# Sorted expert blocks: row transposes moved from TensorE and VectorE to DMA, with four operand buffers and six PSUM banks

## The reference

```python
gate = xf @ Wg + bg                                  # xf: 8192 x 128, 8 experts
topv, topi = jax.lax.top_k(gate, 2)
probs = jax.nn.softmax(topv, axis=-1)
comb = jnp.zeros((N, E)).at[jnp.arange(N)[:, None], topi].set(probs)
h = jax.nn.relu(jnp.einsum('nc,ecf->nef', xf, W1) + b1)   # hidden width 512
y = jnp.einsum('nef,efc->nec', h, W2) + b2
out = jnp.einsum('nec,ne->nc', y, comb)
```

## Time and profile before

| | |
|---|---|
| Median of 3 runs | 2232.34 us (2230.03 to 2232.52) |
| The profiled execution's own time | 2230.25 us |
| Its span in the trace | 2228.3 us |
| PE / DVE / ACT / POOL busy, share of span | 78% / 62% / 53% / 40% |
| Phase 8, first load issued to last scatter issued | 1920.52 us to 2175.8 us of the span |

### The profile page before, as it was taken

How to read it: one execution, slowest core, us unless ns; L and a number is a source line. 1 busy time by engine, 2 the same in 40 slices (tenths; PEclk the granted TensorE clock), 3 DMA queues, 4 the chain that set the end, 5 groups by cost and what they waited for, 6 DMA issues and landing times.

```text
span 2228.3 us, 46761 instructions
## 1 busy us (share of the span) xinstructions
PE 1747.8 (78%) x14634; PEld 956.4 (43%) x14634; DVE 1380.8 (62%) x3633; ACT 1190.7 (53%) x1780; POOL 898.8 (40%) x1789
## 2 busy tenths in 40 slices
PE   2968888888866788877999999999995440499990
PEld 2824444444435233333444444444443430277660
DVE  5445565556547777884666666666664650377766
ACT  1446767676754678752444444444445430388770
POOL 1232323232313233342434443444343477466664
PEclk9999999999975899975999999999996555699995
DMA  5099000000010000000000000000003011122227
GB/s 147 1 335 331 0 0 0 0 0 0 0 48 0 10 0 0 0 38 1 1 0 0 0 0 0 0 0 0 0 1 114 29 54 54 58 88 89 88 75 231
DMA packets 59021, 99.89 MB, mean 45 GB/s; under 512 B 8690, under 2 KB 25970, under 8 KB 57908
## 3 DMA queue, kind: packets, MB, share of 16 engines
q1 hardware_dynamic: 47216, 78.87, 10.8%
q0 software_dynamic: 9088, 18.89, 2.5%
q10 hardware_dynamic: 2628, 1.00, 0.2%
HBM read 38.84 MB, written 59.90 MB: 44 GB/s over the span
## 4 chain that ended last, share of the span: by engine, by line
PE 33%; POOL 6%; DVE 5%; issue 4%; ACT 2%; DVEq 2%; DMA 1%; POOLq 1%; ACTq 0%; SPq 0%
PE OP L1657 7%; POOL h_dram L393 5%; PE OP L1952 5%; PE SP L1937 4%; PE M L1616 4%; PE M L1572 3%; PE M L1586 2%; DVE mx L1042 2%; PE SP L1637 2%; PE M L1612 2%; PE M L1607 2%; ACT shared L637 1%; PE OP L1686 1%; PE M L1927 1%; DVE st L1001 1%
## 5 line engine op out<-in xcount | busy, mean ns | idle before, releaser
L656 ACT ACTIVATE pt<-SP 128x1024 f32<-128x1024 f32 (+1 forms) x512 | 459.7, 921 | 364.9 <-PE SP L1637 364.7
L1657 PE MATMUL OP<-pt,vs 128*32 128x256 f32 (+1 forms) x4096 | 434.4, 362 | 15.4 <-ACT pt L656 13.8
L1042 DVE TENSOR_REDUCE mx<-M 128x2 f32<-128x512 f32 (+1 forms) x384 | 257.0, 690 | 118.1 <-PE M L1616 114.9
L1657 PEld LDWEIGHTS OP<-pt,vs 128*32 128x32 f32 x4096 | 177.0, 110 | 182.6 <-issue 51.3
L475 POOL TENSOR_SCALAR_AFFINE_SELECT pt<-pt 128x256 f32<-128x256 f32 x512 | 196.0, 407 | 0.0
L403 POOL DMA_INDIRECT y_dram<-hT,dest x156 | 150.7, 966 | 108.6 <-DVE hT L1309 72.1
L751 ACT ACTIVATE pt<-SP,b 128x512 f16<-128x512 f32 x156 | 107.2, 687 | 143.0 <-PE SP L1937 116.7
L472 POOL TENSOR_TENSOR spare<-ones 128x1 f32<-128x1 f32 x256 | 49.4, 193 | 309.0 <-ACT pt L656 308.8
L1637 PE MATMUL SP<-shared,ksT 32*128 32x256 f16 (+1 forms) x2048 | 172.0, 262 | 2.4 <-ACT ksT L629 1.2
L1616 PE MATMUL M<-ksT,shared 24*128 24x128 f16 (+1 forms) x1024 | 153.5, 250 | 0.0
L442 POOL TENSOR_TENSOR ha<-hT,ones 128x256 f32<-128x256 f32 x64 | 39.6, 619 | 280.1 <-PE M L1572 270.8
(11 more groups left out here) (267 smaller groups left out, 3330.0 us busy)
## 6 DMA issues: line engine op xcount, KB each, us to landing
h_dram<-shared SPq DMA_DIRECT2D x8, 4488.0 KB, 34.3
hT<-h_dram SPq DMA_DIRECT2D x39, 264.0 KB
rows<-g_dram SPq DMA_DIRECT2D x4, 2048.0 KB, 7.1
pt<-y_dram SPq DMA_DIRECT2D x32, 256.0 KB, 3.7
x_sb<-in_x SPq DMA_DIRECT2D x8, 512.0 KB, 8.9
pt<-in_w SPq DMA_DIRECT2D x4, 1024.0 KB, 7.1
out<-x_sb SPq DMA_DIRECT2D x16, 256.0 KB, 3.0
y_dram<-hT,dest POOLq DMA_INDIRECT x156
```

What stands on the lines that cost most here:

```text
L656: act.activation(pt[:, u % 4, :, 0:W], SP[u % 2][:, :, 0:W], ACT.Exp, scale=SCALE).then_inc(s["exp"], 1)
L1042: dve.tensor_reduce(to, M[:, k % 2, :].rearrange("p (j k) -> p j k", j=2 if k < 8 else 4), AX.X, ALU.max).then_inc(s["mred"], 1)
L1657: last = pe.matmul(OP[32 * g:32 * g + 32, j // 2, c + q0:c + T], vs[:, par, k, HG * j + g, :], pt[:, u % 4, i, k * T:k * T + T - q0], star ...
```

## The change

SP now also issues, for each block, four DMAs with `transpose=True`, each of which turns one row group of 128 rows by 256 16-bit numbers (64 KB) from `xg` into the moving operand. TensorE's eight transposes and VectorE's copy are gone. The operand has four buffers instead of two (two more lie in the tensor `st`). Banks 6 and 7, which the transposes used, join banks 0 to 3 in a ring of six for the first products, taken in turn over all pairs (g, f).

In SP's order the transposes of block g - 1 stand behind the load of block g, so also behind that load's wait for `yE`. They wait for the load of their own block, and from the fifth block on until TensorE has done the first products of the block four before.

```diff
-        hg = ksT[:].rearrange("p a j t -> p (a j t)").rearrange("p (k v n) -> p k v n", k=2, v=2)
+        hg = [half.rearrange("p (k v n) -> p k v n", k=2, v=2)[:, k]
+              for half in (ksT[:].rearrange("p a j t -> p (a j t)"), str_[:].bitcast(F16)) for k in range(2)]
...
-        blk_s = sems("blk", 0, "xT xE hid relu lo y yE dst in0 in1 in2 in3 out0 out1 out2 out3 yin0 yin1 yin2 yin3 sum comb done")
+        blk_s = sems("blk", 0, "hid relu lo y yE in0 in1 in2 in3 out0 out1 out2 out3 yin0 yin1 yin2 yin3 sum comb done turn0 turn1 turn2 turn3")
...
+        def hid_bank(i):
+
+            return bank[(0, 1, 2, 3, 6, 7)[i % 6]]
...
+            def turn_rows(g):
+
+                sp.wait_ge(k[f"in{g % 4}"], 16 * (g // 4 + 1))
+                if g >= 4:
+                    sp.wait_ge(k["hid"], F1 * (g - 3))
+                for r in range(4):
+                    sp.dma_start(hg[g % 4][:, :, r * P:(r + 1) * P], xg[:, g % 4, r, 0:D].bitcast(F16),
+                                 transpose=True).then_inc(k[f"turn{g % 4}"], 16)
+
             for g in range(NBLK):
                 row = sp.value_load(browi[0:1, g:g + 1], min_val=0, max_val=HROWS - BLK)
                 if g >= 4:
                     sp.wait_ge(k["yE"], g - 3)
                 sp.dma_start(xg[:, g % 4].rearrange("p n c -> p (n c)"),
                              h_dram[bass.ds(row, BLK), :].rearrange("(p g) c -> p (g c)", g=4)).then_inc(k[f"in{g % 4}"], 16)
+                if g:
+                    turn_rows(g - 1)
+            turn_rows(NBLK - 1)
...
-                        act.activation(hid1[:, g % 2, f, 0, :], bank[f], ACT.Relu, bias=bias, scale=1.0 / WSCALE)
-                        act.activation(relu[:, f, :], bank[f], ACT.Relu, bias=bias,
+                        of = hid_bank(F1 * g + f)
+                        act.activation(hid1[:, g % 2, f, 0, :], of, ACT.Relu, bias=bias, scale=1.0 / WSCALE)
+                        act.activation(relu[:, f, :], of, ACT.Relu, bias=bias,
                                        scale=1.0 / WSCALE).then_inc(k["relu"], 1)
...
-                def take(g):
-
-                    dve.wait_ge(k["xT"], g + 1)
-                    if g >= 2:
-                        dve.wait_ge(k["hid"], F1 * (g - 1))
-                    dve.tensor_copy(hg[:, g % 2].rearrange("p v n -> p (v n)"), bank[6 + g % 2].bitcast(F16)).then_inc(k["xE"], 1)
...
-                take(0)
                 for g in range(NBLK):
                     targets(g)
-                    low(g, 0)
-                    low(g, 1)
-                    low(g, 2)
-                    if g + 1 < NBLK:
-                        take(g + 1)
-                    low(g, 3)
+                    for f in range(F1):
+                        low(g, f)
                     if g:
                         leave(g - 1)
...
-                def take(g):
-
-                    pe.wait_ge(k[f"in{g % 4}"], 16 * (g // 4 + 1))
-                    if g >= 2:
-                        pe.wait_ge(k["xE"], g - 1)
-                    to = bank[6 + g % 2].bitcast(F16).rearrange("p (v g n) -> p v g n", v=2, g=4)
-                    for r in range(4):
-                        for v in range(2):
-                            last = pe.transpose(to[:, v, r, :], xg[:, g % 4, r, v * D // 2:(v + 1) * D // 2].bitcast(F16), ident16[:])
-                    last.then_inc(k["xT"], 1)
-
                 def hidden(g, f, e):
 
                     if f == 0:
-                        pe.wait_ge(k["xE"], g + 1)
-                    if g:
-                        pe.wait_ge(k["relu"], F1 * (g - 1) + f + 1)
+                        pe.wait_ge(k[f"turn{g % 4}"], 64 * (g // 4 + 1))
+                    i = F1 * g + f
+                    if i >= 6:
+                        pe.wait_ge(k["relu"], i - 5)
                     for n, (u, v) in enumerate(PARTS):
-                        last = pe.matmul(bank[f], w16[1][:, 0, u, bass.ds(e * (F1 * P) + f * P, P)], hg[:, g % 2, v, :],
+                        last = pe.matmul(hid_bank(i), w16[1][:, 0, u, bass.ds(e * (F1 * P) + f * P, P)], hg[g % 4][:, v, :],
                                          start=(n == 0), stop=(n == 2))
                     last.then_inc(k["hid"], 1)
...
-                take(0)
                 e0 = None
...
-                    if g + 1 < NBLK:
-                        take(g + 1)
                     hidden(g, 3, e)
```

## The result

The changed kernel takes 2295.22 us in the median (2292.76 to 2299.68), the kernel before on the same chip 2231.19: a ratio of 1.0289, 95% interval 1.027 to 1.0309. It is 64 us slower; forecast were 32 us slower (2263), within a range of 2213 to 2400. The profiled execution took 2293.29 us, its span 2291.5.

What follows compares the result with a forecast made beforehand. It took phase 8 as bound by TensorE's instruction order; after the change late transposes would set a pitch of 6.92 us. -0.9, +28.1 and +4.0 gave +31.2 us: 2261.5, or 2263.5 on the median, range 2213 to 2400.

Steps and rivals of the forecast that it cites:

- TensorE's share: TensorE's order in phase 8: eight transposes cost 0.45 us per block, so 6.14 falls to 5.69; 17.1 us if TensorE binds.
- The banks and the buffers priced at nothing: First products' bank ring and operand buffers: six banks instead of four buy 0; four buffers only loosen how early transposes land.
- VectorE's copy: Copy after TensorE's transposes, 0.683 us, 39 times: removal priced at nothing, since TensorE's 6.14 us cover VectorE's 4.62.
- The release 2.06 us after the end of the block two before: SP's order: transposes stand behind a load that waits for VectorE's `leave`, so they start 2.06 us after that end.
- The sum: Whole kernel: two pitches gain 0.45 each, 36 lose 0.78 each, the start adds 4.0; together +31.2 us.
- The full clock: TensorE, busy 5.69 of 6.92 us (82%), was expected to keep granted clock 1.00, not the 1.2 GHz level.
- x: SP's queue: distance between two transposing issues, taken as 1.26 us from GpSimd's scatter; break-even at 0.74 with y = 2.3.
- y: Time from a block's last transposing issue to its landing, taken as 2.3 us from a 64 KB scatter.
- The corner "x = 1.26, y = 3.7: P = 7.62": Case of scatter-like issues and slow landing: block pitch P of 7.62 us, 1.48 above today.
- The first two pitches: Start of phase 8: the first three loads wait for nothing, so these pitches gain 0.45 us each.
- Cheap transposes: Rival on SP's issues: x = 0.34, y = 2.3, transposes hidden; -15.9 us, 2216.4; chance 0.35.
- "The DMA engines themselves take longer": Rival: DMA engines need longer for a block's transposes than TensorE for the block; about 2392 us; chance 0.20.

Runs made afterwards that it cites:

- none: The changed kernel with the four transposes left out, so first products read whatever lies in the buffers: 2210.30 us, ratio 0.9907 to the kernel before.
- one_early: The changed kernel with one transposing DMA of 256 KB per block, a separate load of the fields and the looser load wait: 2215.51 us, ratio 0.9922.
- four_banks_again: The changed kernel with four banks instead of six in the ring of the first products, on the usual chip: 2297.96 us, ratio 1.029.
- two_buffers: The changed kernel with two operand buffers instead of four, transposes waiting for the first products of the block two before: 2293.98 us, ratio 1.0284.
- early: The changed kernel with SP's load waiting for its buffer's last reader, `targets(g - 4)`, instead of `leave(g - 4)`: 2259.68 us, ratio 1.0125.
- one_again: The changed kernel with one transposing DMA of 256 KB per block, the load still waiting for `leave(g - 4)`; usual chip: 2255.62 us, ratio 1.0108.
- half: The changed kernel with only two of the four row groups transposed, the other two left out: 2240.73 us, ratio 1.0046.
- eight: The changed kernel with eight transposing DMAs of 128 x 128 per block instead of four of 128 x 256, on the slower chip: 2486.18 us, before 2309.56.

## Why the prediction was right in its direction and wrong in its size

**TensorE's share: right.** 0.45 us per block, 5.69 us left: none and one_early run at 5.70 and 5.69 us.

**The banks and the buffers priced at nothing: right** (four_banks_again, two_buffers). No run tested VectorE's copy alone.

**The release 2.06 us after the end of the block two before: right.** In the changed kernel TensorE passes from one block to the next at 2052.25 and the load's issue ends at 2054.33, 2.08 us later. That this wait stood ahead of the transposes in SP's order was the heart of the forecast; early, one_again and one_early together show that it is, since neither measure alone suffices (2260 and 2256 us) and both together give 2216.

**The sum: too small, and its largest single missing term is the clock.** Follow the chain of waits back from the first products of block 37 (2217.59 us) to those of block 3 (1952.79): 264.8 us for 34 blocks, where the forecast of 6.92 each has 235.3. In 15 places the chain goes through TensorE's work on one block, the release, the issues and the landing, and so covers two blocks; the 4 blocks left over it spends in SP's own order, 6.8 us each. One such pair, in the mean, us:

| piece | forecast | measured |
|---|---|---|
| TensorE's work on a block | 5.69 | 6.54 (7 times 5.69, 8 times 7.27) |
| its end to the end of the load's issue | 2.06 | 2.09 |
| that to the first transposing issue | 0 | 0.11 |
| first to fourth issue (3x) | 3.78 | 4.23 |
| start of the fourth issue to its landing (y) | 2.3 | 2.74 |
| landing to first product | 0 | 0.13 |
| together | 13.83 | 15.84 |

**The full clock: this is the step that failed.** The prediction said "it is busy 5.69 of 6.92 us, 82%, and I expect the full clock", and so put the lower level at nothing. From 1950 to 2200 us the granted clock was 0.95. The lower level came in 8 of the 15 places and cost 1.58 us in each, 12.6 us of the 29.5 by which the chain is longer than forecast. No run takes the lower clock away by itself; early and half keep the full clock, but they change the waits too. So the 12.6 us are read from the trace and not shown by an experiment.

**x and y: the right rows, both somewhat low.** x was to be 1.26 us. The median issue is 1.24, but now and then one takes 2 to 3 us, and the distance of two is 1.35 in the mean of all blocks and 1.41 on the chain: 6.8 us in all. The reason given for x was wrong. I took the scatter as the nearer row because both are cut into many pieces; but an issue of 32 KB costs what one of 256 KB costs, and by the earlier trace rows the plain load is cut no more coarsely than the scatter (1.9 KB a packet against 2.1). y was to be 2.3 us, which the earlier trace rows have from the start of a scatter's issue to its landing, the same two points as y in the sum. It is 2.34 to 3.69 here, 2.6 in the mean, and 2.74 on the chain: another 6.6 us. Landings of blocks that waited, from the chain:

```profile
2010.34 3.25 DMA st<-hT
...
2026.31 2.35 DMA ksT<-hT
...
2059.68 2.63 DMA ksT<-hT
...
2150.14 3.69 DMA ksT<-hT
```

The small pieces of 0.11 and 0.13 us, priced at nothing, make 3.6 us more. So issues, landings and small pieces make 17 us together, and the clock 12.6. The corner "x = 1.26, y = 3.7: P = 7.62" comes close to the measured 7.8 by luck: y is not 3.7, and what it lends to the sum belongs to the clock and to the longer issues. (Its end of the range is also added up wrongly: 36 x 1.48 - 0.9 + 5.4 gives 2290, not 2293.)

**The sum again.** From the first products of the first block to those of the last it is 2223.29 - 1929.75 = 293.5 us, and 2159.49 - 1925.34 = 234.2 us before: 59.4 more. The start is 4.4 us later (4.0 forecast) and the end 0.6 shorter: 63.2, the difference of the two spans. The first two pitches, which were to gain 0.9 us together, lost 0.9: SP's issues for these blocks (1923.33, 1929.66, 1936.37) stand 6.3 and 6.7 us apart, more than TensorE's 5.69, so even without the late release SP's order held them up.

**The rivals.** Cheap transposes fall for the four DMAs of this change, since an issue costs 1.24 us and not 0.34 or anything under 0.74. "The DMA engines themselves take longer" falls too: I had priced a packet at 94 ns. The queue table of the changed kernel from 1930 to 2220 us has

```profile
q1 hardware_dynamic: 48528, 19.85, 31.0%
```

which is 0.310 x 16 x 290 = 1438 us of engine time. The 36 loads take 17 us each of it by the earlier trace rows (0.154 x 16 x 255 / 37), and what is left, 826 us, over 151 transposing DMAs is 5.5 us each, so 22 us per block or 1.4 us on each of 16 engines, against the 6 to 12 us that I allowed. The Trainium skill, "Advanced Engine Details and Errata", section "X-Bar Transpose (TRN2)", calls transposing DMAs as fast as regular ones; for the DMA engines that is roughly so here (1.4 us against 1.1 for a load of about the same bytes), for the queue that issues them it is not. The Trainium skill, "VectorE: DVE Perf Modes", section "The three transpose paths", has 1309 ns for a 128 x 128 transpose by DMA. That is near the issue of 1.23 us for this size in the run eight, but an issue of eight times the size takes 1.32, and from issue to landing one of 128 x 256 takes 2.6 us in the changed kernel.

Not tried: why single issues take 2 us or more, why the clock fell after some waits and not after others, and what part of the 2.6 us from issue to landing is the DMA engines' queueing behind the load.

## What to carry to other kernels

When work is moved to a queue that executes in order, look at what that queue waits for ahead of it: here a load's wait for a late result, stricter than its buffer needed, stood before the transposes. When a change makes a busy engine wait in every block, don't take its full clock for granted: here that was the largest single term missing from the sum. Count every issue of the queue at its mean and not at its median, with the gaps around it, and look in the trace between which two points a latency is measured. And where an issue costs the same for 32 and 256 KB, lay the data out so that one DMA does it; that and the looser wait turned a loss of 64 us into a gain of 16, and neither did so alone.

## What the runs showed of the hardware

- SP's issue of a transposing DMA takes 1.23 us in the median for 32 KB, 1.24 for 64, 1.26 for 128 and 1.32 for 256 KB; a plain load takes 0.34.
- From the start of its issue to its landing, the fourth DMA of 64 KB in a block takes 2.34 to 3.69 us in the changed kernel, 2.6 in the mean. One of 256 KB takes 3.1 to 5.8 us in one_again, 4.0 in the median.
- After waits of 2.0 to 4.4 us TensorE's granted clock was 0.77 over the next block in the case shown, and 8 of 34 blocks took 7.27 us instead of 5.69; after 18 other waits of 0.8 to 3.1 us a block took 5.69.
- One chip ran the same kernels about 3.5% slower (2310 against 2231 us in the kernel before), with TensorE's mean granted clock alike (0.88 to 0.89 in both); the cause is open.
